# A deformable convolution whose offset convolution takes three kernel columns at once

## The chip, the cores and the metric

The kernel runs on one core of one Trainium2 chip. The core has TensorE (matmuls, written into PSUM), VectorE, ScalarE, GpSimd and SyncE, which work side by side and wait for each other by semaphores. The metric is the device time of one execution in microseconds (us).

## The reference

The input x has 4 images of 128 channels and 48 x 48 pixels. Two residual layers follow each other. The change touches the first part of the first one:

```python
x = x + L0(_gn(x))          # _gn: group norm, 32 groups of 4 channels
x = x + L1(_gn(x))          # L1: 3x3 convolution 128 -> 128, bias

# L0
om = conv3x3(x, w_offset)   # 128 -> 27 channels, padding 1
om = om + b_offset
dy, dx, mask = om[:, 0:18:2], om[:, 1:18:2], sigmoid(om[:, 18:])
# for each of the 9 taps: bilinear sample of x at (y + ky - 1 + dy, x + kx - 1 + dx)
cols = bilinear_gather(x, py, px) * mask          # 4 corners each
out = einsum('bckhw,ock->bohw', cols, w_conv) + b_conv
out = relu(batch_norm(out))                        # statistics over all images
```

So each pixel gets 27 numbers from the offset convolution, and by them 9 samples of 4 corners of 128 channels.

## The kernel before, in words

All is float32. Channels lie on the 128 partitions. The 9216 pixels are cut into 24 chunks (six an image) of 384 pixels, which are 8 rows of 48, or 3 tiles of 128 pixels. `xn` holds the normalised image with a border, in rows of 50 columns, two images at a time.

For each chunk c:

- **Offset convolution** (`offset_conv`, line 429): nine matmuls, one a tap, sum into `OM`, 27 partitions of PSUM. The tap's shift is in what is read of `xn`.
- **Copy** (`copy_offsets`, line 599): ScalarE copies `OM` into `om` and adds the bias.
- **Turn** (`turn_offsets`, line 438): three transposes bring pixels onto the partitions, in `OT`, which lies in the same PSUM bank (`OMT`) as `OM`.
- **Indices** (`indices`, line 788): some fifteen short VectorE steps make the rows of a table to fetch (`idx`) and the weights of the corners; ScalarE makes the mask (`masks`).
- **Gathers** (line 377): GpSimd issues 27 indirect DMAs a chunk, each of which brings for one tap and one tile four corners of 128 channels for 128 pixels from a table in HBM.
- **Items**: work then goes by items of three gathers: one tap of three tiles, or in the first and last chunk three taps of one tile (`BY_TILE`). For an item ScalarE scales the first corner (`scale_item`), VectorE weighs the other three and adds all (`sum_item`, lines 858 to 874), TensorE turns the sum back to channels (`turn_item`, line 484), ScalarE copies that (`copy_cols`, line 625), and TensorE multiplies it with the weights two items later (`conv_item`, line 472).

The order of every engine is written out by hand. GpSimd gathers item n only when the item nine before has been summed and item n-4 has been turned (`LEAD`, line 375). The offset convolution of chunk c+2 is dealt out over TensorE's items 3 to 8 of chunk c, its last tap at item 0 of chunk c+1. In chunk 0 the taps of chunk 1 go three at a time before items 0, 1 and 2:

```python
SPREAD = {3: (0,), 4: (1,), 5: (2,), 6: (3,), 7: (4, 5), 8: (6, 7)}
FIRST_SPREAD = {5: (0, 1), 6: (2, 3), 7: (4, 5), 8: (6, 7)}
```

Tap 0 waits until the weights of the chunk before are done, for they are made from the same bank. Copy and turn of chunk c+1 stand at item 1 of chunk c, indices and mask at item 2 (`turn_place`, `index_place`). From chunk 22, item 1, on there is no chunk left to prepare. After the 24 chunks come batch norm, the second group norm and the second convolution.

Of the kernel before, what the change touches and what calls it, by code (L numbers as in the profile page):

```python
# [18 lines left out]
ALL = B * CHUNKS  # L19
# [16 lines left out]
TILE_ROWS = 3  # L36
# [18 lines left out]

SPREAD = {3: (0,), 4: (1,), 5: (2,), 6: (3,), 7: (4, 5), 8: (6, 7)}
FIRST_SPREAD = {5: (0, 1), 6: (2, 3), 7: (4, 5), 8: (6, 7)}
LAST_TAPS = (8,)


def offset_taps(c, i):

    if c == 0 and i < 3:
        return 1, tuple(range(3 * i, 3 * i + 3))
    if i == 0 and c + 1 < ALL:
        return c + 1, LAST_TAPS
    spread = SPREAD if c else FIRST_SPREAD
    if c + 2 < ALL and i in spread:
        return c + 2, spread[i]
    return None, ()  # L70

# [83 lines left out]
def build(nc, x_d, tab_d, woff_d, wconv_d, w1_d, boff_d, par_d, grid_d, out_d):  # L155

    with ExitStack() as ctx:
        def sb(name, shape, dt=F32):
            return ctx.enter_context(nc.sbuf_tensor(name, shape, dt))
# [7 lines left out]
        x = sb("x", [P, B * HW])  # L167
        o = sb("o", [P, B * HW])
        xn = sb("xn", [P, IMAGES * PW, PW])
# [4 lines left out]
        cols = sb("cols", [P, TURNS, CP])  # L174
        woff = sb("woff", [P, TAPS, 27])
        wconv = sb("wconv", [P, TAPS, P])
# [5 lines left out]
        w_plus, w_minus, w_outer = (w_mix[:, i:i + 3, :] for i in (0, 3, 6))  # L182
        boff = sb("boff", [27, 1])
# [4 lines left out]
        om = sb("om", [27, CP])  # L188
        mask = sb("mask", [P, TILES, 9])
# [12 lines left out]
        row = sb("row", [P, TILES, 9])  # L202
# [20 lines left out]
        OMT = ps("OMT")  # L223
# [5 lines left out]
        first = PA[0][:, 0:CP].rearrange("p (u c) -> p u c", c=P)  # L229

        wt = PA[1][:, 0:2 * 4 * TILES * 9].rearrange("p (n q t k) -> p n q t k", n=2, q=4, k=9)
        OM, OT = OMT[0:27, 0:CP], OMT[:, CP:CP + 96]
        VT, UT = VU[0:9, 0:CP], VU[0:9, CP:CP + P]
# [8 lines left out]
        consts = sem("consts")  # L242
# [10 lines left out]
        om_copied = sem("om_copied")  # L253
# [48 lines left out]
        def rows_of(t, start, n):  # L302
            return t[:, start:start + n].rearrange("p (r w) -> p r w", w=W)
# [37 lines left out]
        def _(pl):  # L341
# [64 lines left out]
        def _(pe):  # L406
# [21 lines left out]

            def offset_conv(c, taps=range(TAPS), first=0, rows=ROWS):
# [5 lines left out]
                if taps[-1] == TAPS - 1:  # L435
# [59 lines left out]
            offset_conv(0, first=0, rows=TILE_ROWS)  # L495
            pe.wait_ge(consts, 9)
            turn_offsets(0, (0,))
# [10 lines left out]
            order = all_items()  # L508
            convs = 0
            for c in range(ALL):  # L510
# [3 lines left out]
                for k in range(len(items(c))):  # L514
                    n, taps = offset_taps(c, k)
                    if taps and taps[0] == 0:
# [3 lines left out]
                    if taps:  # L520
                        offset_conv(n, taps)

# [57 lines left out]
        def _(act):  # L580
# [17 lines left out]

            def copy_offsets(part, lo=0, hi=CP):
# [51 lines left out]
            deviation_of(0)  # L651
            act.wait_ge(consts, 11)
# [4 lines left out]
            copy_offsets(0, 0, TILE_ROWS * W)  # L657
            masks(0, 0, 1)
            norm_xn(0, 2)
            copy_offsets(1, TILE_ROWS * W, CP)  # L660
            masks(1, 1, TILES)
            copy_u(0)
# [366 lines left out]
```

## Time and profile before

| | us |
|---|---|
| three runs | 1061.64, 1062.00, 1064.07 |
| median | 1062.0 |
| span of the profiled execution | 1061.3 |
| TensorE busy | 763.8 |
| VectorE busy | 803.4 |
| GpSimd busy | 669.4 |
| ScalarE busy | 378.9 |

The profiled execution's own time is taken as its span; the median of the runs is 0.7 us above it. In the profile PE is TensorE, PEld its weight loads, DVE VectorE, ACT ScalarE, POOL GpSimd. A float32 matmul stands there as two records. The ends of TensorE's matmuls are modelled; in the windows the columns after a stretch and its length are the busy us (and instructions) of PE, PEld, DVE, ACT and POOL, the granted clock of TensorE as a share of 2.4 GHz, the busy share of the DMA engines, and GB/s; a wait that ends by "remote" is one for which the profile found no local instruction that ended then.

### The profile page before, as it was taken

The numbers are of one execution on the slowest core, as the hardware profiler recorded it, in microseconds if no ns is written. First come the engines' busy times: TensorE is split into PE (matmuls) and PEld (weight loads), VectorE is DVE, ScalarE is ACT, GpSimd is POOL, SyncE is SP. The second block draws the span as 40 slices with busy tenths as digits, with TensorE's granted clock in tenths as the row PEclk, the third lists the DMA queues.
The fourth block names the chain that finished last, engine by engine and source line by source line (L and its number), as shares of the span: only waits on it lengthen the run. The fifth ranks groups of instructions, "written<-read, shape, count | busy, mean of one in ns | idle before, by whom it ended". The sixth has DMA issues, their size and how long they took to land.

```text
span 1061.3 us, 8955 instructions
## 1 busy us (share of the span) xinstructions
PE 763.8 (72%) x2436; PEld 354.9 (33%) x2436; DVE 803.4 (76%) x1533; ACT 378.9 (36%) x1026; POOL 669.4 (63%) x731
## 2 busy tenths in 40 slices
PE   6787777676766867666768667674776676579998
PEld 5342222322222222222223223221222222267776
DVE  3788788787878778786878778786888787867664
ACT  2333334433333335333424334332433333343320
POOL 3666666666666666666666666666666667635661
PEclk9677677778768668977867867976878775579999
DMA  8666666666666666666566665666666666630111
GB/s 290 185 171 185 187 191 185 176 189 184 185 178 188 186 183 189 189 189 182 166 185 191 189 187 169 186 186 181 181 186 189 186 188 189 175 113 23 51 50 56
DMA packets 56245, 181.38 MB, mean 171 GB/s; under 512 B 11012, under 2 KB 12036, under 8 KB 55812
## 3 DMA queue, kind: packets, MB, share of 16 engines
q0 software_dynamic: 51840, 169.91, 55.8%
q1 hardware_dynamic: 3924, 10.32, 2.6%
q10 hardware_dynamic: 432, 0.59, 0.2%
q8 instruction: 19, 0.31, 0.1%
q14 instruction: 30, 0.25, 0.1%
HBM read 176.06 MB, written 4.72 MB: 170 GB/s over the span
## 4 chain that ended last, share of the span: by engine, by line
POOL 39%; issue 16%; DVE 16%; PE 14%; another core or an unknown queue 10%; DMA 3%; ACT 2%; DVEq 0%; POOLq 0%; ACTq 0%
POOL g L377 39%; DVE g L858 5%; DMA g<-corner_table,idx 3%; DVE PA L870 2%; DVE PA L872 2%; PE TP L564 2%; PE PA L564 2%; PE CO L564 2%; DVE acc L874 2%; PE OMT L432 2%; PE TP L484 1%; PE VU L564 1%; PE OMT L564 1%; PE CO L472 1%
## 5 line engine op out<-in xcount | busy, mean ns | idle before, releaser
L377 POOL DMA_INDIRECT g<-corner_table,idx x648 | 613.5, 947 | 327.5 <-issue 188.9
L472 PE MATMUL CO<-cols,wcs 128*128 128x384 f32 (+1 forms) x504 | 261.2, 622 | 123.2 <-issue 64.7
L644 ACT ACTIVATE PA<-g,wt 128x128 f32<-128x128 f32 x642 | 203.0, 357 | 400.2 <-DMA g<-corner_table,idx 171.5
L858 DVE TENSOR_TENSOR g<-g,PA 128x1152 f32<-128x1152 f32 (+1 forms) x217 | 291.3, 1342 | 68.6 <-DMA g<-corner_table,idx 58.9
L432 PE MATMUL OMT<-xn,woff 128*27 128x384 f32 (+2 forms) x450 | 208.4, 576 | 43.1 <-DVE wt L828 21.7
L484 PE MATMUL TP<-ident,acc 128*128 128x128 f32 x648 | 145.1, 344 | 118.5 <-DVE acc L874 60.3
L472 PEld LDWEIGHTS CO<-cols,wcs 128*128 128x128 f32 x504 | 94.1, 241 | 285.8 <-issue 186.0
L484 PEld LDWEIGHTS TP<-ident,acc 128*128 128x128 f32 x648 | 92.4, 173 | 261.0 <-DVE acc L874 114.5
L870 DVE TENSOR_TENSOR PA<-g,PA 128x384 f32<-128x384 f32 x214 | 120.3, 562 | 59.6 <-ACT PA L644 22.9
L872 DVE TENSOR_TENSOR PA<-g,PA 128x384 f32<-128x384 f32 x214 | 120.3, 562 | 18.1 <-DVE PA L870 7.6
L874 DVE TENSOR_TENSOR acc<-g,PA 128x384 f32<-128x384 f32 x214 | 118.4, 553 | 15.2 <-DVE PA L872 4.9
L625 ACT ACTIVATE cols<-TP 128x384 f32<-128x384 f32 (+1 forms) x217 | 102.0, 470 | 66.9 <-remote 46.1
L432 PEld LDWEIGHTS OMT<-xn,woff 128*27 128x27 f32 x450 | 39.2, 115 | 109.8 <-issue 78.7
L319 POOL TENSOR_TENSOR g<-xn 128x288 f32<-128x288 f32 (+1 forms) x60 | 41.5, 726 | 31.7 <-ACT xn L719 30.5
L458 PE MATMUL CO<-vt,ut 9*128 9x384 f32 (+1 forms) x56 | 35.6, 730 | 0.0
L797 DVE SCALAR_TENSOR_TENSOR low<-OMT,grid 128x54 f32<-128x54 f32 (+2 forms) x25 | 5.2, 208 | 34.5 <-remote 27.0
L607 ACT ACTIVATE mask<-OMT 128x27 f32<-128x27 f32 (+2 forms) x25 | 4.8, 192 | 62.4 <-remote 23.9
L618 ACT ACTIVATE vt<-VU 9x384 f32<-9x384 f32 x24 | 11.4, 476 | 43.2 <-remote 31.0
L427 PE MATMUL PA<-gavg 128*128 128x128 f32 x128 | 18.2, 306 | 2.9 <-POOL gavg L354 2.6
L447 PE MATMUL VU<-ident,vsum 128*9 128x128 f32 x72 | 16.0, 346 | 4.2 <-issue 4.2
L611 ACT ACTIVATE std<-OMT,eps 128x1 f32<-128x1 f32 x4 | 1.0, 262 | 50.4 <-PE OMT L413 50.4
L311 POOL TENSOR_TENSOR x<-x,o 128x576 f32<-128x576 f32 x8 | 12.1, 1524 | 10.9 <-ACT o L707 10.8
(132 smaller groups left out, 545.8 us busy)
## 6 DMA issues: line engine op xcount, KB each, us to landing
g<-corner_table,idx POOLq DMA_INDIRECT x648, 3.4
out_dram<-x SPq DMA_DIRECT2D x16, 288.0 KB, 2.1
x<-x_dram SPq DMA_DIRECT2D x3, 1152.0 KB, 7.6
x<-x_dram ACTq DMA_DIRECT2D x3, 192.0 KB, 4.0
x<-x_dram SPq DMA_DIRECT2D x3, 192.0 KB, 3.8
wconv<-wconv_dram SPq DMA_DIRECT2D x1, 576.0 KB, 5.0
w<-w_dram SPq DMA_DIRECT2D x1, 576.0 KB
grid<-grid_dram SPq DMA_DIRECT2D x1, 162.0 KB, 4.1
```

The source lines that it names most:

```text
L319: return eng.tensor_tensor(mixed[:, m, first:first + rows, :], p, q, op)
L377: pl.indirect_dma_start(out=g[:, k, t].rearrange("p q c -> p (q c)"), out_offset=None, in_=tab_d, in_offset=bass.IndirectOffsetOnAxis(ap=i ...
L432: last = nc.tensor.matmul(OM[:, first * W:(first + rows) * W], woff[:, k, :], xn[:, row + k // 3:row + k // 3 + rows, k % 3:k % 3 + W], st ...
L472: last = nc.tensor.matmul(co_bank(c, t)[:, t * P:t * P + size], wcs[:, c // CHUNKS % 2, k, :], cols[:, s % TURNS, n * P:n * P + size], sta ...
L484: last = nc.tensor.transpose(TP[s % 2][:, n * P:(n + 1) * P], acc[:, s % SUMS, n, :], ident[:])
L564: last = nc.tensor.matmul(MX[h % 2][m][:, 0:HB], w, mixed[:, m, r:r + BR, :], start=(ky == 0), stop=(ky == 2))
L625: nc.scalar.activation(cols[:, s % TURNS, 0:size], TP[s % 2][:, 0:size], ACT.Copy).then_inc(copied, 1)
L644: last = nc.scalar.activation(first[:, n] if s < LAST_SUMS else g[:, k, t, 0, :], g[:, k, t, 0, :], ACT.Copy, scale=wt0[:, c % 2, t, k:k + 1])
L858: nc.vector.tensor_tensor(corners[:, :, 1:4, :], corners[:, :, 1:4, :], weights[:, :, 1:4].unsqueeze(3).to_broadcast([P, size, 3, P]), ALU ...
L870: nc.vector.tensor_tensor(some, corners[:, :, 1, :], some, ALU.add).then_inc(sum_step, 1)
L872: nc.vector.tensor_tensor(some, corners[:, :, 2, :], some, ALU.add).then_inc(sum_step, 1)
L874: nc.vector.tensor_tensor(acc[:, s % SUMS, 0:size, :], corners[:, :, 3, :], some, ALU.add).then_inc(sum_step, 1)
```

## The change

A row of the kernel (three taps) becomes one matmul. Its weights are 96 columns: three slots of 32, one for each kernel column, with 27 in use. It reads whole bordered rows of 50 columns, so it has 8 x 50 = 400 columns, and leaves three partial sums in partitions 0, 32 and 64 on, each of which belongs to pixels shifted by one column. ScalarE copies the three slots apart, each with its shift (columns x to x+47 of every row), into one tile `om` of 96 partitions. The turn is no longer a transpose but a matmul with `pick`, a 96 x 27 matrix of zeros and three ones a column, which adds the three slots while it turns. `pick` is made by GpSimd at the start. One matmul of the new offset convolution for chunk c+2 stands before item 5 of chunk c, one before item 7, and the last before item 0 of chunk c+1.

```diff
-SPREAD = {3: (0,), 4: (1,), 5: (2,), 6: (3,), 7: (4, 5), 8: (6, 7)}
...
+FIRST_KROW, SECOND_KROW, LAST_KROW = 5, 7, 0
+
+
+def offset_row(c, i):
+
+    if c == 0 and i < KROWS:
+        return 1, i
+    if i == LAST_KROW and c + 1 < ALL:
+        return c + 1, KROWS - 1
+    if c + 2 < ALL and i in (FIRST_KROW, SECOND_KROW):
+        return c + 2, (FIRST_KROW, SECOND_KROW).index(i)
+    return None, None
...
-        OM, OT = OMT[0:27, 0:CP], OMT[:, CP:CP + 96]
+        OM, OT = OMT[0:SLOTS, 0:PCP], OMT[:, PCP:PCP + TILES * SLOT]
...
+            pl.memset(pick[:], 0.0).then_inc(consts, 1)
...
+            for x in range(KCOLS):
+                pl.wait_ge(consts, 12 + x)
+                pl.affine_select(out=pick[:], in_=pick[:], compare_op=ALU.not_equal, fill=1.0, base=-SLOT * x,
+                                 pattern=[[-1, OFFSETS]], channel_multiplier=1).then_inc(consts, 1)
...
-                for k in taps:
-                    last = nc.tensor.matmul(OM[:, first * W:(first + rows) * W], woff[:, k, :],
-                                            xn[:, row + k // 3:row + k // 3 + rows, k % 3:k % 3 + W],
-                                            start=(k == 0), stop=(k == TAPS - 1))
...
+                for k in krows:
+                    last = nc.tensor.matmul(OM[:, first * PW:(first + rows) * PW], woff[:, k, :], xn[:, row + k:row + k + rows, :],
+                                            start=(k == 0), stop=(k == KROWS - 1))
...
-                    last = nc.tensor.transpose(OT[:, 32 * t:32 * t + 27], om[:, t * P:(t + 1) * P], ident[0:27, 0:27])
+                    last = nc.tensor.matmul(OT[:, SLOT * t:SLOT * t + OFFSETS], om[:, t * P:(t + 1) * P], pick[:], start=True, stop=True)
...
-                nc.scalar.activation(om[:, lo:hi], OM[:, lo:hi], ACT.Identity, bias=boff[:]).then_inc(om_copied, 1)
+                for x in range(KCOLS):
+                    slot = slice(SLOT * x, SLOT * (x + 1))
+                    source = OM[slot, lo * PW:hi * PW].rearrange("p (r w) -> p r w", w=PW)[:, :, x:x + W]
+                    last = nc.scalar.activation(rows_of(om[slot, :], lo * W, (hi - lo) * W), source, ACT.Identity, bias=boff[slot, :])
+                last.then_inc(om_copied, 1)
```

TensorE's program before, in chunk 1 from the turn of chunk 2's offsets (L441) over items 2 to 5 (OMT<-xn,woff is the offset convolution, TP the turn of an item, CO its convolution):

```order
L441 MATMUL OMT<-ident,om 128x27 x3
L458 MATMUL CO<-vt,ut 128x384
L472 MATMUL CO<-cols,wcs 128x384
L484 MATMUL TP<-ident,acc 128x128 x3
L432 MATMUL OMT<-xn,woff 27x384
L472 MATMUL CO<-cols,wcs 128x384
L484 MATMUL TP<-ident,acc 128x128 x3
L432 MATMUL OMT<-xn,woff 27x384
L472 MATMUL CO<-cols,wcs 128x384
```

The same place of TensorE's program after the change:

```order
L448 MATMUL OMT<-pick,om 128x27 x3
L465 MATMUL CO<-vt,ut 128x384
L479 MATMUL CO<-cols,wcs 128x384
L491 MATMUL TP<-ident,acc 128x128 x3
L479 MATMUL CO<-cols,wcs 128x384
L491 MATMUL TP<-ident,acc 128x128 x3
L479 MATMUL CO<-cols,wcs 128x384
L491 MATMUL TP<-ident,acc 128x128 x3
L440 MATMUL OMT<-xn,woff 96x400
```

The taps before items 3 and 4 are gone, and the first matmul of chunk 3's offsets stands before item 5; it is one of 96 output rows and 400 columns in place of three of 27 and 384.

ScalarE's program before, from the end of item 1 of chunk 1 to item 2 (PA<-g,wt is the scaling of an item, with the semaphores it waits for):

```order
L644 ACTIVATE PA<-g,wt 128x128 [waits sum_step,gathered1]
L644 ACTIVATE PA<-g,wt 128x128 x2
L625 ACTIVATE cols<-TP 128x384 [waits turned]
L601 ACTIVATE om<-OMT,boff 27x384 [waits om_ready]
L644 ACTIVATE PA<-g,wt 128x128 [waits sum_step,gathered2]
```

And after the change:

```order
L655 ACTIVATE PA<-g,wt 128x128 [waits sum_step,gathered1]
L655 ACTIVATE PA<-g,wt 128x128 x2
L636 ACTIVATE cols<-TP 128x384 [waits turned]
L611 ACTIVATE om<-OMT,boff 32x384 [waits om_ready]
L611 ACTIVATE om<-OMT,boff 32x384 x2
L655 ACTIVATE PA<-g,wt 128x128 [waits sum_step,gathered2]
```

Between the copy of the turned sums and the scaling of item 2 there are three copies now instead of one.

## Rows read from the trace of the kernel before

**Rows 1.** The page: span, busy time and instructions of each engine, chain by engine.

```profile
span 1061.3 us, 8955 instructions
...
PE 763.8 (72%) x2436; PEld 354.9 (33%) x2436; DVE 803.4 (76%) x1533; ACT 378.9 (36%) x1026; POOL 669.4 (63%) x731
...
POOL 39%; issue 16%; DVE 16%; PE 14%; another core or an unknown queue 10%; DMA 3%; ACT 2%; DVEq 0%; POOLq 0%; ACTq 0%
```

**Rows 2.** Groups by line: engine, tiles, shapes, xcount | busy us, mean ns | idle before.

```profile
L377 POOL DMA_INDIRECT g<-corner_table,idx x648 | 613.5, 947 | 327.5 <-issue 188.9 <-remote 99.1 <-PE TP L484 23.7
...
L472 PE MATMUL CO<-cols,wcs 128*128 128x384 f32 x396 | 239.7, 696 | 107.1 <-issue 55.1 <-ACT cols L625 49.8
...
L432 PE MATMUL OMT<-xn,woff 128*27 128x384 f32 x414 | 202.2, 598 | 41.9 <-DVE wt L828 21.7 <-issue 17.4 <-remote 2.8
...
L601 ACT ACTIVATE om<-OMT,boff 27x384 f32<-27x384 f32 x23 | 12.9, 559 | 3.0 <-issue 1.9 <-remote 1.1
...
L441 PE MATMUL OMT<-ident,om 27*128 27x27 f32 x72 | 11.5, 270 | 1.2 <-ACT om L601 1.2
```

**Rows 3.** Windows from pause to pause of GpSimd: stretch, us, busy and instructions by engine.

```profile
412.23:433.73 21.50, 15.74 (x56) 6.67 (x54) 18.39 (x39) 10.72 (x26) 14.19 (x15) 0.84 0.63 183
433.73:455.25 21.52, 11.66 (x40) 4.29 (x40) 16.44 (x24) 7.91 (x24) 14.19 (x15) 0.92 0.63 184
455.25:481.40 26.15, 18.55 (x51) 7.33 (x52) 22.06 (x42) 9.83 (x29) 17.04 (x19) 0.81 0.63 181
876.36:905.94 29.58, 17.45 (x41) 8.16 (x42) 20.43 (x42) 10.10 (x31) 19.88 (x22) 0.56 0.65 186
```

**Rows 4.** The same windows, line 432 (offset convolution) alone.

```profile
412.23:433.73 21.50, 3.02 (x8) 0.59 (x6) 0.84 0.63 183
433.73:455.25 21.52, 4.61 (x12) 0.94 (x12) 0.92 0.63 184
...
876.36:905.94 29.58, 0.00 (x0) 0.00 (x0) 0.56 0.65 186
```

**Rows 5.** Timeline of GpSimd around a pause: start us, us, ..., [idle before <-releaser].

```profile
451.24 0.95 POOL L377 DMA_INDIRECT g<-corner_table,idx  x1 [0.31 <-issue]
455.25 0.94 POOL L377 DMA_INDIRECT g<-corner_table,idx  x1 [3.07 <-remote]
```

**Rows 6.** Timeline of all engines around that pause.

```profile
446.93 0.55 PE L484 MATMUL TP<-ident,acc 128*128 128x128 f32 x3 [0.83 <-issue]
...
455.02 0.49 ACT L625 ACTIVATE cols<-TP 128x384 f32<-128x384 f32 x1 [2.77 <-remote]
...
455.40 0.56 ACT L601 ACTIVATE om<-OMT,boff 27x384 f32<-27x384 f32 x1
...
455.56 1.65 PE L472 MATMUL CO<-cols,wcs 128*128 128x384 f32 x2 [4.28 <-ACT cols L625]
...
456.83 0.56 DVE L870 TENSOR_TENSOR PA<-g,PA 128x384 f32<-128x384 f32 x1 [0.40 <-ACT PA L644]
```

**Rows 7.** Timeline of chunk 10: copy of offsets, item 2's scaling, turn, first index step.

```profile
415.87 0.56 ACT L601 ACTIVATE om<-OMT,boff 27x384 f32<-27x384 f32 x1
...
418.49 0.95 ACT L644 ACTIVATE PA<-g,wt 128x128 f32<-128x128 f32 x3 [2.06 <-DMA g<-corner_table,idx]
...
418.52 0.52 PE L441 MATMUL OMT<-ident,om 27*128 27x27 f32 x3
...
421.61 0.21 DVE L797 SCALAR_TENSOR_TENSOR low<-OMT,grid 128x54 f32<-128x54 f32 x1
```

**Rows 8.** Timeline of the start and of chunk 0.

```profile
14.08 0.37 ACT L601 ACTIVATE om<-OMT,boff 27x144 f32<-27x144 f32 x1 [0.61 <-PE OMT L432]
...
27.19 4.04 PE L432 MATMUL OMT<-xn,woff 128*27 128x384 f32 x6
...
33.49 0.94 POOL L377 DMA_INDIRECT g<-corner_table,idx  x1 [2.44 <-PE TP L484]
...
47.66 0.21 DVE L797 SCALAR_TENSOR_TENSOR low<-OMT,grid 128x54 f32<-128x54 f32 x1 [4.53 <-remote]
```

More of the change, by code:

```diff
@@ L52, in conv_lag @@
     return 1 if c in BY_TILE else 2
-SPREAD = {3: (0,), 4: (1,), 5: (2,), 6: (3,), 7: (4, 5), 8: (6, 7)}
[L57 to L70, printed above, removed]
+KROWS, KCOLS, SLOT = 3, 3, 32
+OFFSETS = 27
+SLOTS = KCOLS * SLOT
+PCP = ROWS * PW
+FIRST_KROW, SECOND_KROW, LAST_KROW = 5, 7, 0
[7 more added lines that the diff above has]
+    return None, None
 SHIFT_SUMS = (2, 3, 4)
@@ L174, in build @@
         cols = sb("cols", [P, TURNS, CP])
-        woff = sb("woff", [P, TAPS, 27])
+        woff = sb("woff", [P, KROWS, SLOTS])
         wconv = sb("wconv", [P, TAPS, P])
@@ L182, in build @@
         w_plus, w_minus, w_outer = (w_mix[:, i:i + 3, :] for i in (0, 3, 6))
-        boff = sb("boff", [27, 1])
+        boff = sb("boff", [SLOTS, 1])
         params = sb("params", [P, 4])
@@ L187, in build @@
         gavg = sb("gavg", [P, P])
-        om = sb("om", [27, CP])
+        om = sb("om", [SLOTS, CP])
+        pick = sb("pick", [SLOTS, OFFSETS])
         mask = sb("mask", [P, TILES, 9])
@@ L427, in warm_up, with offset_conv @@
                     nc.tensor.matmul(bank[:, 0:P], gavg[:], gavg[:], start=True, stop=True)
-            def offset_conv(c, taps=range(TAPS), first=0, rows=ROWS):
+            def offset_conv(c, krows=range(KROWS), first=0, rows=ROWS):
                 row = c // CHUNKS % IMAGES * PW + c % CHUNKS * ROWS + first
-                for k in taps:
-                    last = nc.tensor.matmul(OM[:, first * W:(first + rows) * W], woff[:, k, :],
-                                            xn[:, row + k // 3:row + k // 3 + rows, k % 3:k % 3 + W],
-                                            start=(k == 0), stop=(k == TAPS - 1))
-                if taps[-1] == TAPS - 1:
+                for k in krows:
+                    last = nc.tensor.matmul(OM[:, first * PW:(first + rows) * PW], woff[:, k, :], xn[:, row + k:row + k + rows, :],
+                                            start=(k == 0), stop=(k == KROWS - 1))
+                if krows[-1] == KROWS - 1:
                     last.then_inc(om_ready, 1)
@@ L495, in _ @@
             offset_conv(0, first=0, rows=TILE_ROWS)
-            pe.wait_ge(consts, 9)
+            pe.wait_ge(consts, 15)
             turn_offsets(0, (0,))
@@ L514, in _ @@
                 for k in range(len(items(c))):
-                    n, taps = offset_taps(c, k)
-                    if taps and taps[0] == 0:
+                    n, krow = offset_row(c, k)
+                    if krow == 0:
                         pe.wait_ge(wt_ready, part_count(n - 1))
                         pe.wait_ge(xn_ready, 2 * (n // CHUNKS) + XN_PARTS)
-                    if taps:
-                        offset_conv(n, taps)
+                    if n is not None:
+                        offset_conv(n, (krow,))
                     while convs <= first_item(c) + k - conv_lag(c) and (c, k) != (ALL - 1, len(items(c)) - 1):
@@ L597, in copy_u, with copy_offsets @@
                 nc.scalar.activation(ut[:, b % 2, :], UT, ACT.Copy).then_inc(u_copied, 1)
-            def copy_offsets(part, lo=0, hi=CP):
+            def copy_offsets(part, lo=0, hi=ROWS):
                 act.wait_ge(om_ready, part + 1)
-                nc.scalar.activation(om[:, lo:hi], OM[:, lo:hi], ACT.Identity, bias=boff[:]).then_inc(om_copied, 1)
+                for x in range(KCOLS):
[3 more added lines that the diff above has]
+                last.then_inc(om_copied, 1)
             def masks(part, lo=0, hi=TILES):
@@ L651, in _ @@
             deviation_of(0)
-            act.wait_ge(consts, 11)
+            act.wait_ge(consts, 12)
             norm_xn(0, 0)
@@ L656, in _ @@
             act.wait_ge(wo_in, 32)
-            copy_offsets(0, 0, TILE_ROWS * W)
+            copy_offsets(0, 0, TILE_ROWS)
             masks(0, 0, 1)
             norm_xn(0, 2)
-            copy_offsets(1, TILE_ROWS * W, CP)
+            copy_offsets(1, TILE_ROWS, ROWS)
             masks(1, 1, TILES)
@@ L1010 @@
     corners = [tokens[:, y:y + SIDE, z:z + SIDE] for y in range(2) for z in range(2)]
+    woff = taps_first(np.asarray(L0_conv_w_offset)[order]).reshape(P, KROWS, KCOLS, OFFSETS)
+    woff = np.pad(woff, ((0, 0), (0, 0), (0, 0), (0, SLOT - OFFSETS)))
     arrays = {
@@ L1013 @@
         "corner_table": np.ascontiguousarray(np.stack(corners, axis=3)).reshape(B * TABLE, 4 * P),
-        "woff_dram": taps_first(np.asarray(L0_conv_w_offset)[order]),
+        "woff_dram": np.ascontiguousarray(woff.reshape(P, KROWS, SLOTS)),
         "wconv_dram": taps_first(np.asarray(L0_conv_w_conv)),
         "w1_dram": taps_first(np.asarray(L1_conv_weight)),
-        "boff_dram": np.ascontiguousarray(np.asarray(L0_conv_b_offset)[order]).reshape(27, 1),
+        "boff_dram": np.pad(np.asarray(L0_conv_b_offset)[order], (0, SLOTS - OFFSETS)).reshape(SLOTS, 1),
         "par_dram": np.ascontiguousarray(np.stack([np.asarray(v) for v in (
```

## The prediction

> **What bounds the kernel now.** I read the page first, then the groups of instructions, then windows laid from one pause of GpSimd to the next, and last the timeline around one pause.
>
> The page says: span 1061.3 us; TensorE is busy for 763.8 us of it, VectorE 803.4, GpSimd 669.4, and the chain that ended last runs over GpSimd's gathers with 39% (and 16% "issue", the gaps between them) [rows 1]. So no engine is full, and the gathers lead. The groups say what a gather costs: 947 ns of GpSimd, with 327.5 us of idle time before the 648 of them [rows 2]. Of that idle time 0.30 us stands before each one (648 x 0.30 = 194 us) [rows 5]; some 133 us are left, of which 99.1 lie in waits that the profile puts down to "remote" and 23.7 in waits for the turned sums (TP) [rows 2].
>
> An item of work is three gathers: 3 x (0.95 + 0.30) = 3.75 us. The timeline shows how they go: fifteen at that pace, then a pause of 3.07 us [rows 5]. The reader is to see that the pauses are regular. From pause to pause five items take 21.50 and 21.52 us, six take 26.15, seven take 29.58: 4.30, 4.30, 4.36 and 4.23 us an item [rows 3]. The pause grows with the number of items before it, as if it caught up a debt. DMA moved 181 to 186 GB/s in all four. I take this, 4.2 to 4.3 us an item, for the pace of the gather path, whatever ends the single pause.
>
> Is it TensorE's pace? The first two stretches have 8 and 12 records of the offset convolution, 3.02 and 4.61 us of TensorE; the last (chunk 22, after which no chunk is left to prepare) has none at all [rows 4]. It is TensorE's easiest stretch, 17.45 busy us in 29.58, and it still takes 4.23 us an item. This is the row on which the forecast rests. It is a stretch of its own with a longer run, so I don't read its 0.07 us as zero; they are a rival below.
>
> What ends a pause looks like TensorE all the same: GpSimd, before item n, waits (line 375) until item n-4 is turned. The turn of one item was recorded at 446.93, for 0.55 us; ScalarE's copy of it started only at 455.02 (2.77 us of waiting, "remote"), and GpSimd at 455.25 [rows 5, 6]. TensorE had been idle for 4.28 us by then, since its next matmul waits for that copy [rows 6]. So the signal came late, not the work. A shorter list of matmuls doesn't cure what an idle TensorE doesn't cure.
>
> **The change part by part.** Sums are made against the profiled execution, 1061.3 us; the median of the three runs, 1062.0, is 0.7 above it.
>
> Offset matmuls. 225 matmuls (two records each, 450: 414 of 384 columns of 598 ns and 36 shorter) become 75 with 150 records of up to 400 columns. The trace has none that fills 96 output rows. The nearest rows are the 27-row one, 598 x 400/384 = 623 ns, and the 128-row one, 696 x 400/384 = 725 ns [rows 2]; I take 650, near the first, since it reads the same tile. TensorE's work falls by about 210 - 150 x 0.63 = 115 us, 5 us a chunk. Behind it lies the gather pace, so the loop gets 0 of it. Also gone is TensorE's stop before item 3, where tap 0 waits for the weights of the next chunk: the first row now stands before item 5. That stop lay before work that nobody waited for; 0.
>
> The turn. Three transposes of 270 ns [rows 2] become three ordinary matmuls over 96 rows with 27 columns, with two records each: 0.27 to 0.54 us for one, so at most 0.8 us more a chunk. It sits after item 1. In chunk 10 the turn was recorded from 418.52 for 0.52 us, and VectorE reads it at 421.61, after its own item: 2.57 us to spare [rows 7]. Cost 0; without that cover 0.8 a chunk. Here a rule of the Trainium skill speaks against the change: "TensorE: Matmul & The Clock Gate", Terms, gives transpose mode as four times faster for FP32. By that rule the three would go from 0.81 to 3.24 us, 2.4 more. By the row's spare time that too would just fit, and the sum would stay as it is. No run so far shows it.
>
> ScalarE's slices. One copy of 559 ns [rows 2] becomes three of 384 elements. Neither a copy from partition 32 or 64 nor one that skips two columns a row is in the trace. By the distance at which two copies follow each other (455.02 to 455.40, and 0.56 for the last) three take 0.38 x 2 + 0.56 = 1.3 us at the least and 3 x 0.56 = 1.7 at the most [rows 6]; I take 1.6, so 1.1 us more a chunk and some 25 us on ScalarE, which is busy for 7.91 to 10.72 us in the stretches of [rows 3]. Queued behind the slices is item 2's scaling, for which VectorE's second step waits. In chunk 10 the copy began at 415.87 and would end at 417.5, before the scaling at 418.49 and the turn at 418.52 [rows 7]. Nothing moves: 0. Where a late signal has held ScalarE (455.02, copy 455.40) VectorE already waited for it, 0.40 us at 456.83 [rows 6], and would wait 1.1 more. GpSimd is four items ahead there, so the gather pace covers this; if it did not, see the second rival.
>
> Start. The first copy of offsets waited 0.61 us for TensorE [rows 8]. The first convolution gets shorter by more than that, but two more slices of 0.3 us follow: 0, between -0.6 and +0.3. The constants on GpSimd are five short instructions at about 3 us, while its first gather is issued at 16.19; 0. Before item 0's turn stand three taps of chunk 1, 4.04 us at the half clock; one row of two records takes 1.4. The first pause, 2.44 us, ends at 33.49 with that turn [rows 8]. The gain is between 0 and 2.4; I take 1, since the sums of item 0 are ready only shortly before its turn.
>
> Run lengths. Pauses come after four to seven items by chance and timing, and longer runs are a little cheaper. An easier TensorE gets its signals out no later: -0.5, between -3 and +3.
>
> Sum: 1061.3 - 1 - 0.5 = 1059.8, and 0.7 to the median: **1060.5 us**.
>
> **The rivals.** First, faster: the late signals do hang on how much TensorE has to do. For it: the pauses end with TensorE's signals, and the stretch without offset work has the longest run. If every stretch came to 4.23 instead of 4.30, 216 items would gain 15 us; two thirds of the offset work go, so 10, and with all the pauses (133 us) shrinking like the TensorE records of a chunk (71 to 62, 13%) it would be 17. Time 1044 to 1051, say 1048. Against it: the seven-item stretch, and equal times of 21.50 and 21.52 us with 3.02 and 4.61 us of offset work [rows 3, 4].
>
> Second, slower: the slices hold item 2. One mechanism: between items 1 and 2 ScalarE's copies end later than VectorE's first step on item 2, whose second step waits for the scaling. It decides once this delay (1.1 us, and up to 0.8 for the turn behind) is no longer covered by the gathers in flight, which is when the om_turned signal too is late; VectorE stood 4.5 us for it in chunk 0 [rows 8]. If 22 chunks paid 1.1 us it would be 24 us; with the third of them in which a pause falls there, 8 us. Time 1069, with 1066 to 1073 around it.
>
> Third, slower: the clock. In the stretch without offset work the granted clock was 0.56, in the others 0.81 to 0.92 [rows 3]. If the loop goes to that, an item's convolution takes 1.65 us [rows 6] instead of 2 x 0.70 on the mean [rows 2], still inside 4.3 us an item. It costs where TensorE leads: the last chunk and the entry into the second convolution, some four items and a few warm-up matmuls, 3 to 5 us: 1066. The Trainium skill says the same in "TensorE: Matmul & The Clock Gate", Part 1, "What's actually happening": "the default state is throttled, and activity releases the throttle". The trace agrees; but chunks 22 and 23 run the same matmuls before and after, so I give it little.
>
> That the change doesn't do what it says I exclude: the order shows one matmul per row of 96x400.
>
> **How the numbers follow.** A measurement of this kernel can tell about 0.3% from no change, 3.2 us. The forecast has 0.64, with its own range of 1056 to 1065; inside it a third lies below 1058.8 and a tenth above 1065.2. The faster rival has 0.13, the slices 0.14, the clock 0.09. Faster: 0.64 x 0.32 + 0.13 = 0.33. Slower: 0.64 x 0.08 + 0.14 + 0.09 x 0.5 = 0.24. Same: 0.43. Range for 8 in 10: 1052 to 1067.
>
> **What would show it.** Right: TensorE's busy time near 670 us and ScalarE's near 404, and gathers from pause to pause still at 4.2 to 4.35 us an item, with pauses of 2.5 to 4 us. The offset-turn row has 144 records. VectorE's first index step (low) waits no longer in sum than before. Wrong: fewer or shorter pauses at the same run length (first rival); ScalarE's scaling of item 2 starting late in most chunks with VectorE waiting for it (second); a granted clock of 0.5 from 940 us on (third).

## The result

The changed kernel takes 1070.9 us (median of 20 runs, 1063.1 to 1076.8), the kernel before 1063.2 on the same chip (20 runs, 1061.6 to 1066.4). The ratio is 1.0069, with a 95% interval of 1.0051 to 1.0086: slower by some 7 us. The forecast, 1060.5 with a range of 1052 to 1067, was wrong in its sign and left the time outside. The runs of after also spread more, over 13.7 us against 4.8; the quickest, 1063.1, is no slower than before's median. Three of the twelve runs of a kernel below, g4 (1085.2 to 1085.7 us), count as slow and are left out of its ratio; with them its median would stand at 1.0065 of before.

The profiled execution of after took 1070.3 us, with a span of 1068.5. Its page, in the lines of [rows 1]:

```profile
span 1068.5 us, 8556 instructions
...
PE 720.8 (67%) x2208; PEld 400.1 (37%) x2208; DVE 801.4 (75%) x1533; ACT 407.9 (38%) x1076; POOL 669.6 (63%) x735
...
DVE 31%; POOL 20%; PE 16%; issue 14%; another core or an unknown queue 10%; DMA 5%; ACT 4%; DVEq 0%; ACTq 0%; POOLq 0%
```

TensorE is 43 us less busy than in [rows 1], ScalarE 29 us more (408 against the 404 forecast), and the span is 7.2 us longer. The chain that ended last runs more over VectorE than over GpSimd here, but not in a profile of the same kernel on another chip (e6 below: GpSimd 33%, VectorE 20%), so nothing is built on it.

The groups that answer to [rows 2] (xcount | busy us, mean ns | idle before), with the two that read the turned offsets:

```profile
L385 POOL DMA_INDIRECT g<-corner_table,idx x648 | 613.1, 946 | 332.5 <-issue 184.0 <-remote 96.0 <-PE TP L491 37.3
...
L479 PE MATMUL CO<-cols,wcs 128*128 128x384 f32 x396 | 269.6, 776 | 180.3 <-ACT cols L636 92.4 <-issue 87.6
...
L440 PE MATMUL OMT<-xn,woff 128*96 128x400 f32 x138 | 91.7, 761 | 1.8 <-issue 1.8
L611 ACT ACTIVATE om<-OMT,boff 32x384 f32<-32x384 f32 x69 | 39.1, 567 | 1.5 <-remote 0.9
...
L448 PE MATMUL OMT<-pick,om 96*128 96x27 f32 x144 | 27.7, 335 | 4.0 <-ACT om L611 3.5 <-issue 0.4
...
L808 DVE SCALAR_TENSOR_TENSOR low<-OMT,grid 128x54 f32<-128x54 f32 x23 | 4.9, 211 | 49.8 <-remote 48.3 <-issue 1.5
L618 ACT ACTIVATE mask<-OMT 128x27 f32<-128x27 f32 x23 | 4.4, 193 | 92.8 <-DVE pos L809 63.3 <-remote 16.3 <-issue 13.1
```

The offset convolution went from 202 to 92 us, with 761 ns a record where I took 650; the records of the main convolution grew too, from 696 to 776 ns [rows 2], because the mean granted clock fell from 0.78 to 0.68. A slice costs 567 ns, so the copies are what I took them for. What is new is that VectorE's first index step (low) waits 49.8 us, against 27.0 in before:

```profile
L797 DVE SCALAR_TENSOR_TENSOR low<-OMT,grid 128x54 f32<-128x54 f32 x23 | 4.8, 210 | 27.0 <-remote 27.0
```

In 13 of the 23 chunks it waits for the turn, in before in 8. The second pair of profiles (e6 is after, e5 before, on one other chip) repeats this, with 53.4 us against 18.0:

```profile
L808 DVE SCALAR_TENSOR_TENSOR low<-OMT,grid 128x54 f32<-128x54 f32 x23 | 4.9, 211 | 53.4 <-remote 50.8 <-issue 2.5
```

```profile
L797 DVE SCALAR_TENSOR_TENSOR low<-OMT,grid 128x54 f32<-128x54 f32 x23 | 4.8, 210 | 18.0 <-remote 18.0
```

The gathers wait 37.3 us for turned sums in place of 23.7 [rows 2], but this doesn't repeat: it is 26.5 in e6 and 31.8 in e5.

From pause to pause of GpSimd, as in [rows 3] (stretch, length, busy us and instructions of PE, PEld, DVE, ACT, POOL, granted clock, DMA share, GB/s):

```profile
469.41:490.90 21.49, 12.17 (x32) 5.47 (x32) 18.61 (x38) 7.53 (x23) 14.19 (x15) 0.66 0.61 183
490.90:512.31 21.41, 12.20 (x35) 5.74 (x35) 17.33 (x36) 9.80 (x29) 14.19 (x15) 0.66 0.63 184
512.31:537.95 25.64, 14.96 (x39) 7.09 (x39) 20.45 (x29) 9.43 (x28) 17.01 (x18) 0.70 0.63 185
765.29:795.64 30.35, 19.59 (x50) 9.58 (x51) 22.82 (x44) 12.34 (x35) 19.84 (x21) 0.61 0.63 182
```

Five, five, six and seven items: 4.30, 4.28, 4.27 and 4.34 us each. The pace of the regular stretches is as before. The time is lost outside them, little by little: chunk 1's first gather comes 0.2 us later than in before, chunk 12's 3.0, chunk 23's 4.0, the last gather ends 5.6 us later and the last sums 7.2. What follows them takes 111.0 us in both. The 1.6 us between 5.6 and 7.2 are the last items' at a lower clock: from the end of the last gather to the end of the last sums before takes 5.9 us at a granted clock of 1.00, after 7.5 at 0.77. GpSimd's pauses of over 1 us, up to the last item, add up to 134.3 us in place of 129.4. Six of them, not four, follow only one item after another pause, as the second one here in chunk 0; but f3 below, which is faster than before, has ten of these, so their number doesn't measure the cost:

```profile
45.92 0.94 POOL L385 DMA_INDIRECT g<-corner_table,idx  x1 [1.27 <-remote]
...
51.00 0.94 POOL L385 DMA_INDIRECT g<-corner_table,idx  x1 [1.63 <-remote]
```

The place where the change bites is item 2 of a chunk. The timeline of after, one chunk in the middle (start, us, engine, line):

```profile
575.25 1.73 ACT L611 ACTIVATE om<-OMT,boff 32x384 f32<-32x384 f32 x3
...
577.25 0.90 PE L491 MATMUL TP<-ident,acc 128*128 128x128 f32 x3 [0.20 <-issue]
577.61 1.35 DVE L869 TENSOR_TENSOR g<-g,PA 128x1152 f32<-128x1152 f32 x1 [0.41 <-DMA g<-corner_table,idx]
577.61 0.95 ACT L655 ACTIVATE PA<-g,wt 128x128 f32<-128x128 f32 x3 [0.63 <-DMA g<-corner_table,idx]
...
577.95 1.32 PE L448 MATMUL OMT<-pick,om 96*128 96x27 f32 x6
...
579.20 1.64 PE L465 MATMUL CO<-vt,ut 9*128 9x384 f32 x2
...
580.77 1.65 PE L479 MATMUL CO<-cols,wcs 128*128 128x384 f32 x2
...
582.22 0.85 PE L491 MATMUL TP<-ident,acc 128*128 128x128 f32 x3
...
582.39 0.22 DVE L808 SCALAR_TENSOR_TENSOR low<-OMT,grid 128x54 f32<-128x54 f32 x1 [1.58 <-remote]
...
582.82 0.19 ACT L618 ACTIVATE mask<-OMT 128x27 f32<-128x27 f32 x1 [3.74 <-remote]
```

The three slices end at 576.98, and item 2's scaling waits for its data, not for them: here my cover held. So it does elsewhere: the scaling starts right behind the copies in 4 of 23 chunks, in before in 5. The turn is another matter. From the turning of item 1's sums (577.25) to that of item 2's (582.22) TensorE is busy for all of 4.97 us, with turn (1.32), first and main convolution; the gathers deliver an item every 4.28. And the turn, recorded as over at 579.27, is read by VectorE only at 582.39, after 1.58 us of waiting, and by ScalarE after 3.74.

### The profile page after: what moved, and what is told of

It reads as the page before. It is cut to its first block, busy times and chain, and to the rows that moved or that the text cites. A ratio compares the mean times of both kernels' runs of the same rounds, so it can differ in the third digit from the quotient of the medians.

```text
span 1068.5 us, 8556 instructions
## 1 busy us (share of the span) xinstructions
PE 720.8 (67%) x2208; PEld 400.1 (37%) x2208; DVE 801.4 (75%) x1533; ACT 407.9 (38%) x1076; POOL 669.6 (63%) x735
## 4 chain that ended last, share of the span: by engine, by line
DVE 31%; POOL 20%; PE 16%; issue 14%; another core or an unknown queue 10%; DMA 5%; ACT 4%; DVEq 0%; ACTq 0%; POOLq 0%
POOL g L385 20%; DVE g L869 10%; DVE PA L883 5%; DMA g<-corner_table,idx 5%; DVE PA L881 5%; DVE acc L885 4%; PE TP L491 3%; PE CO L479 2%; PE TP L571 2%; PE PA L571 2%; PE CO L571 2%; ACT PA L655 2%; PE VU L571 1%; PE OMT L571 1%
## 5 line engine op out<-in xcount | busy, mean ns | idle before, releaser
L479 PE MATMUL CO<-cols,wcs 128*128 128x384 f32 (+1 forms) x504 | 294.1, 692 | 196.2 <-issue 98.7
L491 PE MATMUL TP<-ident,acc 128*128 128x128 f32 x648 | 165.6, 384 | 134.2 <-DVE acc L885 69.0
L479 PEld LDWEIGHTS CO<-cols,wcs 128*128 128x128 f32 x504 | 111.5, 274 | 308.6 <-issue 174.1
L491 PEld LDWEIGHTS TP<-ident,acc 128*128 128x128 f32 x648 | 103.7, 192 | 302.7 <-DVE acc L885 136.4
L440 PE MATMUL OMT<-xn,woff 128*96 128x400 f32 (+2 forms) x150 | 95.4, 738 | 3.0 <-issue 1.8
L611 ACT ACTIVATE om<-OMT,boff 32x384 f32<-32x384 f32 (+2 forms) x75 | 41.5, 554 | 2.5 <-remote 0.9
L618 ACT ACTIVATE mask<-OMT 128x27 f32<-128x27 f32 (+2 forms) x25 | 4.8, 192 | 95.5 <-DVE pos L809 66.1
L440 PEld LDWEIGHTS OMT<-xn,woff 128*96 128x96 f32 x150 | 32.0, 246 | 6.2 <-issue 3.5
L448 PEld LDWEIGHTS OMT<-pick,om 96*128 96x128 f32 x144 | 28.4, 285 | 5.6 <-issue 3.4
L448 PE MATMUL OMT<-pick,om 96*128 96x27 f32 x144 | 27.7, 335 | 4.0 <-ACT om L611 3.5
```

What stands on the lines that cost most here:

```text
L440: last = nc.tensor.matmul(OM[:, first * PW:(first + rows) * PW], woff[:, k, :], xn[:, row + k:row + k + rows, :], start=(k == 0), stop=(k ...
L448: last = nc.tensor.matmul(OT[:, SLOT * t:SLOT * t + OFFSETS], om[:, t * P:(t + 1) * P], pick[:], start=True, stop=True)
L479: last = nc.tensor.matmul(co_bank(c, t)[:, t * P:t * P + size], wcs[:, c // CHUNKS % 2, k, :], cols[:, s % TURNS, n * P:n * P + size], sta ...
L491: last = nc.tensor.transpose(TP[s % 2][:, n * P:(n + 1) * P], acc[:, s % SUMS, n, :], ident[:])
```

## The experiments

Each was timed against the kernel before on its own chip. The medians of before on the five chips were 1071.9 (the first four runs), 1073.6 (the next four), 1063.6 (f1 to f4), 1072.3 (g1 to g4) and 1073.0 us (h1, h2), so only ratios are compared. "Alone" means put into the kernel before.

**First set: each part alone.** The rivals were the relief of TensorE, the copies, the turn, and the clock.

e1 leaves out six of the nine taps, in the loop over them:

```
+                    if k not in (0, 4, 8):
+                        continue
```

> The kernel before with six of the nine taps of the offset convolution left out (taps 0, 4 and 8 stay where they were), so the offsets are others, and with nothing of the rest of the change. TensorE's relief alone. The slices' theory (ScalarE's two further copies delay the turn of the offsets, and VectorE waits for it): no change, within 2 us of the kernel before, the sum of VectorE's waits before its first index step near the 34 us of before. The clock's theory (fewer matmuls, lower granted clock, every turn and convolution later): the granted clock falls from 0.78 to about 0.68, and the time rises by 5 to 8 us, as the whole change did. The turn's theory: no change.

e2 makes two more copies into spare tiles, ahead of the copy of the offsets:

```
+                act.wait_ge(spared, 2 * part)
+                for i in range(2):
+                    nc.scalar.activation(spare[:, i, lo:hi], OM[:, lo:hi], ACT.Identity, bias=boff[:]).then_inc(spared, 1)
```

> The kernel before with ScalarE's copy of the offsets made three times, twice into spare tiles first, then the real one. TensorE's work is as before. The slices' theory: 4 to 8 us slower, VectorE's waits before its first index step up from 34 us to 50 or more, granted clock near 0.77. The clock's and the turn's theories: within 2 us of the kernel before.

e3 turns the offsets by ordinary matmuls:

```
-  last = nc.tensor.transpose(OT[:, 32 * t:32 * t + 27], om[:, t * P:(t + 1) * P], ident[0:27, 0:27])
+  last = nc.tensor.matmul(OT[:, 32 * t:32 * t + 27], om[:, t * P:(t + 1) * P], ident[0:27, 0:27], start=True, stop=True)
```

> The kernel before with the turn of the offsets as three ordinary matmuls (27 rows) in place of three transposes. The turn's theory: 144 records of about 0.3 us, 0.5 us a chunk more, and 3 us or more in the time. The slices' and the clock's theories: within 2 us of the kernel before.

e4, in after, puts two matmuls of zero weights behind each matmul of a row:

```
+                    for i in range(2):
+                        last = nc.tensor.matmul(OM[:, first * PW:(first + rows) * PW], zeros[:], xn[:, row + k:row + k + rows, :],
+                                                start=False, stop=(k == KROWS - 1 and i == 1))
```

> The changed kernel with two more matmuls of zero weights behind each of its three, which add nothing: TensorE has nearly its old load again, the three copies and the turn as matmul stay. The clock's theory: granted clock back to about 0.77, and the time back to that of the kernel before, within 2 us. The slices' and the turn's theories: it stays 5 to 8 us slower than before, though the clock is back.

Measured: e1 0.9948 (0.9931 to 0.9966), at a granted clock of 0.677; e2 1.0018 (1.0001 to 1.0035); e3 1.0015 (0.9996 to 1.0035); e4 1.0130 (1.0094 to 1.0165), clock 0.763. TensorE's relief (its shorter work) is worth 5 us and not nothing. The clock doesn't cost: in e1 it falls as far as in after and the time falls too, in e4 it comes back and the time gets worse. What e4 adds is load on TensorE, and the gathers show it, as a wait for turned sums of 58.1 us:

```profile
L387 POOL DMA_INDIRECT g<-corner_table,idx x648 | 613.1, 946 | 345.9 <-issue 178.3 <-remote 97.2 <-PE TP L496 58.1
```

With -5.2, +1.8 and +1.5 thousandths the parts alone make -1.9, not +6.9: something costs in place what it doesn't cost alone.

**Second set: in place.** e5 and e6 are both kernels as they are, on one chip, for their profiles. e7 takes two slices out of after (`om` is set to zero at the start, and two kernel columns are lost):

```
-                for x in range(KCOLS):
+                for x in range(1):
```

e8 puts before's nine taps where after has its rows:

```
+SPREAD = {5: (0, 1, 2), 7: (3, 4, 5)}
+FIRST_SPREAD = SPREAD
+LAST_TAPS = (6, 7, 8)
```

> The kernel before, unchanged, for its trace beside the others of this set. Every theory: a ratio of 1, and in the trace gathers at 4.25 to 4.35 us an item.

> The changed kernel, unchanged, beside the parts below on the same chip. Six taps fewer alone were 5.4 us faster (0.9948), three copies alone 1.2 to 1.9 us slower (1.0018), the turn as matmuls alone as much (1.0015). If parts add up, this would be at 0.998 and not at the 1.007 first measured; if something that none of the three holds costs (matmuls of 96 rows out, taps in threes, the slices after late signals), it is at 1.005 to 1.009 again.

> The changed kernel with ScalarE copying only the first of the three slots; the other two stay zero, so the offsets lack two kernel columns. The slices' theory (in the changed kernel they cost more than alone): back to 0.998 or below. The order's theory (three taps' worth of work at a time before items 5, 7 and 0) and the width's theory (96 rows out cost TensorE): it stays within 3 us of the changed kernel, near 1.004 to 1.007.

> The kernel before with its nine taps dealt out three before item 5, three before item 7 and three before the next chunk's item 0, which is where the changed kernel has its matmuls. The order's theory: slower by 4 to 10 us, with GpSimd's waits for the turned sums up from 24 us. The slices' and the width's theories: within 2 us of the kernel before, or a little faster, since the stop before item 3 is gone.

Measured: e5 1074.05 us in its one run; e6 1.0071 (1.0047 to 1.0095), so the result holds on a second chip; e7 1.0033 (1.0008 to 1.0058); e8 1.0038 (1.0017 to 1.0059). The same matmuls in heaps of three cost 4 us: the gathers in e8 wait 44.6 us for turned sums, against 31.8 in e5 (one profile each; that of e8 is of its slowest run, 1084.9 us for a median of 1078.1). A heap, in its timeline:

```profile
598.19 0.90 PE L484 MATMUL TP<-ident,acc 128*128 128x128 f32 x3 [2.51 <-DVE acc L874]
599.02 3.43 PE L432 MATMUL OMT<-xn,woff 128*27 128x384 f32 x6
602.38 0.91 PE L472 MATMUL CO<-cols,wcs 128*128 128x384 f32 x2
```

From 598.19 to 603.29 TensorE is busy with one item, 5.10 us. e7 left a gap: the relief (e1) with one slice should be near 0.995 and was 1.0033. Width, place or turn had to be the difference.

**Third set: width, place, turn.** f2 is e1 (six taps out) with weights of 96 columns (`woff` as `[P, 3, 96]`, zero-padded). f4 is e1 with e8's table. f3 is e7 with

```
-  last = nc.tensor.matmul(OT[:, SLOT * t:SLOT * t + OFFSETS], om[:, t * P:(t + 1) * P], pick[:], start=True, stop=True)
+  last = nc.tensor.transpose(OT[:, SLOT * t:SLOT * t + OFFSETS], om[0:OFFSETS, t * P:(t + 1) * P], ident[0:OFFSETS, 0:OFFSETS])
```

and f1 is after with

```
-    if c + 2 < ALL and i in (FIRST_KROW, SECOND_KROW):
+    rows_at = (FIRST_KROW if c == 0 else 3, SECOND_KROW)
+    if c + 2 < ALL and i in rows_at:
```

> The kernel before with only taps 0, 4 and 8 of the offset convolution (so the output isn't the reference's), as in e1, but each matmul now puts out 96 partitions (its weights padded with zero columns) in place of 27. Places, width of the moving data and the turn are those of e1, which was 0.9948 of before. Theory A (the width in the output partitions costs nothing, since a matmul's record goes by its columns): 0.9948, 0.993 to 0.997, matmul records of 731 ns as in e1. Theory B (96 weight columns are loaded and put out more slowly, and this is part of what after lost): 0.998 or above, weight loads of the line longer than in e1.

> The kernel before with only taps 0, 4 and 8 (so the output isn't the reference's), as in e1 (0.9948), but the three stand where after has its rows: at items 5 and 7 and at item 0 of the next chunk. Theory A (the place costs, since the first matmul comes two items later): 0.998 to 1.001, that is 3 to 6 us over e1. Theory B (in e8 it was the bunches of three that cost, 1.7 us at a time, and one matmul at each place costs nothing): 0.9948, 0.993 to 0.997.

> After with one slice copied, as in e7 (1.0033), and the turn as the three transposes of 27 rows that before had, so that the shifted columns are left out (the output isn't the reference's). Theory A (the turn over 96 rows as ordinary matmuls with their own weights is what is left of the cost): 0.997 to 1.000, offset-turn records back to 72. Theory B (the turn costs nothing beside the rest; the place or the 400 columns are what is left): 1.002 to 1.004.

> After, with the first row of the offset convolution at item 3 of a chunk in place of item 5 (in chunk 0 it stays at 5), where before had its first tap. Theory A (the place costs): 1.002 to 1.005, some 2 to 5 us under after's 1.007. Theory B (slices and turn cost, the place does not): 1.006 to 1.008. Theory C (at item 3 TensorE waits for the mask of the chunk ahead before it may write the bank): above 1.009, with a wait of the line's first matmul that after doesn't show.

Measured: f2 0.9970 (0.9954 to 0.9987), f4 0.9971 (0.9954 to 0.9989), f3 0.9963 (0.9945 to 0.9980), f1 1.0070 (1.0042 to 1.0098). Neither width nor place makes the gap; each may cost up to 2 thousandths over e1, which these intervals can't tell from nothing. f3 has the wide matmuls of 400 columns at after's places and is 3.7 thousandths under before: the relief survives the rearrangement (3.7 or 5.2 thousandths, the intervals don't tell), and only the turn separates it from e7.

**Fourth set: what of the turn.** All four on one chip. g1 keeps the whole change and puts `om` and `pick` into bfloat16. g2 is f3 with its three slices back. g3 is f3 with the turn as an ordinary matmul of `om[0:OFFSETS]` with `ident`. g4 is f3 with each transpose issued twice (`for _ in range(2):`). Like f3, g2, g3 and g4 leave the shifted columns out of the offsets.

> After with the buffer om and the matrix pick in bfloat16 (three slices copied, turn over 96 rows, offsets rounded to bfloat16 before they are summed). Theory A (what costs in after is the time of the turn on TensorE, 1.32 us a chunk at the lower clock, in front of the next item's work): the turn falls to under 0.6 us a chunk and the ratio to 0.996 to 1.001. Theory B (the three slices on ScalarE or the placing are what costs): 1.004 to 1.007. Rival C (an ordinary matmul signals late, whatever its length): 1.004 to 1.007 with waits of VectorE for the turn as in after, 53 us.

> After with its three slices copied, but the turn as three transposes of the first 27 rows (the shifted columns are left out of the sum; the output isn't the reference's). With one slice the same kernel (f3) was 0.9963. Theory A (the turn costs, the slices next to nothing): 0.996 to 0.998. Theory B (slices cost 0.0038, as e7 against e6 has it): 0.999 to 1.001.

> f3 with its turn as ordinary matmuls of the first 27 rows (two records each) in place of transposes; one slice, shifted columns left out (the output isn't the reference's). Theory A (length, or kind, of the matmul): 1.001 to 1.004, as e7 (1.0033), turn about 1.3 us. Theory B (the 96 rows are the cost): 0.996 to 0.998.

> f3 with each of its three transposes of a chunk issued twice, so the turn takes about twice its 0.52 us without being an ordinary matmul (the output isn't the reference's). Theory A (length): 1.000 to 1.003. Theory B (the kind of the matmul, two passes each with its weights): 0.996 to 0.998.

Measured: g1 0.9980 (0.9966 to 0.9995), g2 0.9977 (0.9962 to 0.9992), g3 1.0048 (1.0024 to 1.0072), g4 1.0033 (1.0007 to 1.0059). The turn's group in g1, g2, g3 and g4, in this order:

```profile
L449 PE MATMUL OMT<-pick,om 96*128 96x27 bf16 x72 | 6.7, 195 | 4.3 <-ACT om L612 3.9 <-issue 0.4
```

```profile
L448 PE MATMUL OMT<-ident,om 27*128 27x27 f32 x72 | 11.6, 272 | 4.4 <-ACT om L611 4.4
```

```profile
L448 PE MATMUL OMT<-ident,om 27*128 27x27 f32 x144 | 30.7, 352 | 1.8 <-ACT om L611 1.8
```

```profile
L449 PE MATMUL OMT<-ident,om 27*128 27x27 f32 x144 | 17.8, 263 | 1.8 <-ACT om L612 1.8
```

This separates much. It isn't the 96 rows: g3 has 27 and is slow, g1 has 96 and is fast. It isn't the ordinary matmul: g4 has transposes and is slow, g1 has ordinary ones and is fast. What is left is how much TensorE has to do in a turn: 6.7 and 11.6 us in all are harmless, 17.8 and 30.7 are not. g3 and g4 came out just above what their expectations gave for the length of the turn (1.0048 for 1.001 to 1.004, 1.0033 for 1.000 to 1.003).

One rival stands untested: the number of records. Every slow turn has 144 and every harmless one 72, so time and number rise together, and no run holds one and changes the other. The sizes speak for caution too: g4's turn takes some 6 us more than f3's in all, and the ratio rises by 7 thousandths, over 7 us; g3's takes some 19 us more, and it rises by 8.5. The cost also comes and goes from run to run. The runs of after, e7, f1, g3 and g4 spread over 13 to 17 us, those of f3, g1, g2 and h2 over 5 to 9, and of the former the quickest is at or below before's median but for f1 (1.0008 of it).

And g1, which computes everything that the reference does (offsets rounded to bfloat16 before their sum), turns the change from 7 us slower into 2 us faster than before.

Against the timeline of after, g1's at its turn in the same chunk:

```profile
573.02 0.90 PE L492 MATMUL TP<-ident,acc 128*128 128x128 f32 x3 [0.20 <-issue]
573.72 0.29 PE L449 MATMUL OMT<-pick,om 96*128 96x27 bf16 x3
573.93 1.64 PE L466 MATMUL CO<-vt,ut 9*128 9x384 f32 x2
575.50 1.65 PE L480 MATMUL CO<-cols,wcs 128*128 128x384 f32 x2
576.95 0.85 PE L492 MATMUL TP<-ident,acc 128*128 128x128 f32 x3
```

At the same clock (0.50 of full in both stretches) the item takes 3.93 us from turning to turning where after has 4.97, and the gathers' 4.28 lie between them. Over all 23 chunks, with the medians of the turn and of this stretch, and the number of chunks in which the stretch is over 4.28 us:

| kernel | slices | turn, us | turning to turning, us | chunks over 4.28 | low waits, us | ratio |
|---|---|---|---|---|---|---|
| g1 | 3 | 0.29 | 3.92 | 6 | 33.4 | 0.9980 |
| f3 | 1 | 0.52 | 4.17 | 9 | 30.4 | 0.9963 |
| g2 | 3 | 0.52 | 4.17 | 8 | 32.1 | 0.9977 |
| g4 | 1 | 0.84 | 4.49 | 18 | 66.1 | 1.0033 |
| e7 | 1 | 1.32 | 4.96 | 18 | 46.7 | 1.0033 |
| g3 | 1 | 1.48 | 5.13 | 18 | 46.4 | 1.0048 |
| after | 3 | 1.32 | 4.96 | 19 | 49.8 | 1.0069 |

In these seven kernels, and in f1, e6 and h2 too: with a median under 4.28 us they are faster than before, over it slower. That the crossing of the gather pace is the mechanism is my inference from this order, not shown. The heap of 5.10 us in e8 agrees with it. e3 doesn't fit well: alone in before the same stretch is 5.07 us long, over 4.28 in 17 chunks (before: 4.17, 11 chunks), and the cost only 1.5 thousandths (up to 3.5).

**Last set: is it the short turn alone?** h1 is before with a turn in bfloat16 (27 rows, a 27x27 unit matrix). h2 is g1 with f1's places.

> The kernel before with its buffer om (27 rows) and a 27x27 unit matrix in bfloat16, the turn as three ordinary matmuls, one record each; the nine taps as they are. Theory A (in before the turn's 0.52 us is short enough, and a shorter one brings nothing): 0.999 to 1.001. Theory B (the turn's length counts at any size, so g1's gain is the bfloat16 turn's alone): 0.996 to 0.998.

> g1 (after with its turn in bfloat16, 0.998 of before) with the first row at item 3 of a chunk in place of 5, except in chunk 0. Theory A (the earlier place is worth what e1 against f4 suggests): 0.995 to 0.997. Theory B (the place is worth nothing, as f1 against after has it): 0.997 to 0.9995.

Measured: h1 0.9999 (0.9984 to 1.0015), h2 0.9971 (0.9956 to 0.9985). In before a shorter turn brings nothing that can be measured, so g1's gain over before is taken for the relief of TensorE. h2, the best version that computes everything, is 3 us faster than before and 10 us, by the ratios, than after. Whether its place adds to g1 the intervals don't tell.

## Why the prediction was wrong

**Offset matmuls: wrong, to the good side.** "The loop gets 0 of it" was read from one stretch without offset work that kept 4.23 us an item [rows 3, 4]. The pace inside regular stretches indeed didn't move, in after either. But the relief is worth 3.7 to 5.2 thousandths, 4 to 5.5 us (f3, e1): with the pace unchanged it must lie elsewhere. Part of it lies in chunk 0, by the first gather of chunk 1, one profile each: at 54.5 us in e1, against 56.3 and 56.2 in e2 and e3 on its chip, and at 53.0 in f3, against 57.2 in before on another chip. The rest, I take it, lies in where and how often pauses fall, which windows laid from pause to pause can't show. The first rival had this sign, and priced it at some 13 us (1048 for 1060.5), two to three times what the runs show. Two slips of the working matter little: the 133 us of pauses also hold the 12.9 us before the very first gather, and the 115 us of relief are reckoned with 630 ns a record and not with the 650 taken.

**The turn: the step that failed.** "It sits after item 1. [...] 2.57 us to spare [rows 7]. Cost 0; without that cover 0.8 a chunk." The length was right: 1.32 us for 0.52, 0.8 more. The cost is not 0. From g2 (0.9977) to after (1.0069) it is 9 thousandths, some 10 us, about 0.4 us for each of the 23 chunks. I weighed the turn only against VectorE's reading of it, in one chunk where that came late anyway; in 8 of before's 23 chunks VectorE already waited for the turn, 27.0 us in all, and there was nothing to spare. What counted, by the inference above, was the whole list of TensorE between two turnings of sums, which I never added up: it stood at 4.17 us, next to the 4.2 to 4.3 that I had myself named as the pace, so 0.8 more carried it over. The Trainium skill, in "TensorE: Matmul & The Clock Gate", Terms, gives four times for transpose mode in FP32; at equal shape (27 rows, 27 columns) g2 and g3 show 11.6 and 30.7 us, 2.6 times. Its sign was the right warning, and I let it pass on the spare time of a single chunk.

**ScalarE's slices: nearly right.** Length right (1.73 us a chunk, 1.6 taken). In place two of them cost 1.4 thousandths beside a short turn (g2 less f3) and 3.8 beside the long one (e6 less e7, one chip), alone 1.8 (e2); the intervals overlap in each pair. That is 1.5 to 4 us, against the 0 of the sum. The second rival's mechanism, slices that hold item 2, isn't what happened (4 chunks of 23, before 5). Its other clause, the turn behind them and VectorE's longer wait, points at what did, but its 1069 was reckoned from the slices' 1.1 us in a third of the chunks: that it came out near is luck.

**The clock: right that it falls, wrong as the cause.** 0.684 in after, 0.677 in e1, which is faster than before. TensorE's busy time shows it: 720.8 us and not the 670 foretold, since at the lower clock the main convolution took 30 us more (269.6 for 239.7) and the turning of the sums 20 more (165.6 for 145.1), and this by itself cost nothing. The place that the third rival named, the last items, did cost 1.6 us in the profile of after; but it comes and goes: that stretch takes 7.5 us in e2, e3 and h1 too, which have all of before's offset matmuls, and 5.9 in e7 and f1, which have after's. The clock has one indirect part: at the lower of the two levels (1.2 GHz) the turn takes 1.3 to 1.5 us, at the upper 0.75 to 0.85, and 15 of after's 23 turns are of the long kind.

**Start and run lengths: wrong, small.** Chunk 0 of after:

```profile
28.45 1.54 PE L440 MATMUL OMT<-xn,woff 128*96 128x400 f32 x2
...
33.70 0.95 POOL L385 DMA_INDIRECT g<-corner_table,idx  x1 [2.24 <-remote]
...
47.81 0.21 DVE L808 SCALAR_TENSOR_TENSOR low<-OMT,grid 128x54 f32<-128x54 f32 x1 [3.75 <-remote]
```

The row took 1.54 us for the three taps' 4.04, and the pause still ended at 33.70 instead of 33.49 [rows 8]: 0.2 us of gain in the pause for the 1 us taken, and the first gather comes 0.4 us later than before, at 16.6. VectorE's wait for the turn of chunk 1's offsets is 3.75 us for 4.53 [rows 8]. The run lengths, -0.5, went the other way, +4.9 us in the pauses.

**The sum as measured:** relief with one slice -3.7 (f3), two more slices +1.4 (g2), turn +9.2 (after less g2), together +6.9 thousandths. The three are differences along one row of kernels, so their sum is the result by construction; each carries 2 to 3 thousandths of doubt.

**Still open.** Why the long turn costs 8.5 thousandths in the relieved kernel (g3 less f3) and 1.5 in before (e3). Whether the time of the turn or its number of records counts, and why the cost differs so much from run to run. And why some signals of TensorE come late at all, below.

## What to carry to other kernels

Add up what an in-order engine does between two of its recurring signals, item by item and at its slower clock, and hold each sum against the pace of the loop; an engine that is busy for 70% on the mean may have one item that is over it, and in these kernels more work in that item cost time although the mean fell. When work moves between forms, put the saving and its by-product in separate experiments: here a sound saving of 4 us was hidden under 10 us of a turn that had been priced at 0. A cover read from one chunk is no cover; look at the chunk where it is thinnest.

## What the runs showed of the hardware

A float32 matmul that isn't a transpose is two records and, with 27 columns, 2.6 times a transpose; in bfloat16 over 96 rows it is one of 195 ns.

ScalarE reads from partition 32 or 64, leaving out two columns of 50 a row, at 567 ns for 384 elements, against 559 for the plain copy from 27 partitions [rows 2].

TensorE's records end before others may go on. After's turn ends at 579.27 in the record and is read at 582.39 by a VectorE that waited. In g4 the wait for the turn reaches 66.1 us over 23 chunks, 2.9 us each:

```profile
L809 DVE SCALAR_TENSOR_TENSOR low<-OMT,grid 128x54 f32<-128x54 f32 x23 | 4.9, 211 | 66.1 <-remote 66.1
```

The Trainium skill says why the record need not show it: in "Perfetto Trace Analysis", "Tensor Engine Instruction (MATMUL, LD_WEIGHTS)", "the TE profile time is a model, not a measurement". The trace agrees so far as it goes; it doesn't show what TensorE does in those 3 us.

One kernel on five chips, and on that of the result, had medians from 1063 to 1074 us, more than the whole effect studied: a ratio against the same chip is the only measure here.
